# Binning: ranks summed on TensorE into one column per edge, copied out by ScalarE instead of reduced by VectorE

## The chip, the cores and the metric

The kernel runs on one core of a Trainium2 chip. The core has five engines that run their own instruction streams and meet at semaphores: TensorE (matrix products, written PE), VectorE (DVE), ScalarE (ACT), GpSimd (POOL) and SyncE (SP, which here issues the DMAs). The metric is the device time of one execution in microseconds.

## The reference

Two graph layers over 6250 nodes with 128 features and 200000 edges, sorted by destination. Cut to what matters:

```python
hij = concatenate([h[src], h[dst]]);  e = leaky_relu(hij @ w, 0.2) @ a
att = exp(e) / segment_sum(exp(e), src)[src]
x   = layernorm(x + segment_sum(h[src] * att, dst))          # layer 0
s   = exp(leaky(H_s[src] + H_t[dst]) - max)                  # layer 1, 4 heads
agg = segment_sum(s / (denom[src] + 1e-8) * H[dst], src) + x @ residual_projection
x   = layernorm(x + elu(agg))
```

Gathers and segment sums run over edges. The kernel first sorts the edges into bins, so that both become products with one-hot matrices.

## The kernel before, in words

The program runs through stages: constants, **binning** (`bin_windows`, line 109), edge scores, layer 0, norm and projection, layer 1, and the last norm. A stage ends with a barrier, so what it saves moves all that follows.

Binning goes over 49 windows of 4608 edges, 36 edges on each of 128 partitions. Nodes are in 49 blocks of 128. For each edge it needs the rank: the position of the edge among the edges of its window with the same source block. The rank of an edge is a sum of two parts: the count of edges in its block on the partitions above (*base*), and the count of equal keys among the edges before it on its own partition. One window n takes these steps:

- ScalarE `spread_key` (372, 376): copies the window's block numbers, each repeated 7 times, and its keys, each repeated 18 times, so that VectorE can compare runs.
- VectorE `find` (202, 210, 213): a one-hot of 49 blocks per edge (`bin_onehot`) and the equal-key table (`bin_same`).
- TensorE `base` (278): 36 matmuls add the one-hots of the partitions above; ScalarE `take_base` (382) copies the sum out.
- VectorE `pick` (223): one-hot times base, 36 x 49 numbers per partition (`bin_picked`), one of the 49 not zero.
- TensorE `rank` (288 to 306): with the identity as weights it adds the picked bases and the equal keys into PSUM. Seven columns per edge are kept: the 49 blocks are folded into 7 columns by seven matmuls of 252 columns, and the keys go into six or three of these columns, by ten matmuls.
- VectorE `sum_rank` (231): a reduction over the 7 columns, 252 numbers to 36 per partition, into `bin_rank_sum`.
- ScalarE `spread_rank` (402) repeats the ranks of 28 edges 8 times for VectorE `place` (238), which compares them with 128 lanes into `bin_lanes`. The ranks of the last 8 edges go through ScalarE itself, `measure_ranks` (388) and `place_late` (396).
- VectorE `fold` (245): one-hot times the two payloads (`bin_payload`). TensorE `fill` (317): 36 matmuls of lanes and payload put each edge into its slot. ScalarE `take_raw` (411, 412), TensorE `turn` (324), ScalarE `take_bytes` (418, 419), and SyncE stores the rows.
- Beside it, the projection of the node features runs block by block: `turn_x`, `project`, `take_off` on TensorE, `take_x`, `take_high`, `take_low` on ScalarE.

The windows are pipelined by an order that is written out by hand. In turn n VectorE does `find(n+2)`, `pick(n+1)`, `place(n)`, `fold(n)`, `sum_rank(n+1)`, and in every seventh turn `place_keys` for the seven windows to come. TensorE does `fill(n-1)`, `base(n+2)`, `turn_x(n+2)`, `take_off(n)`, `rank(n+1)`, `turn(n-1)`, `project(n+1)`. ScalarE does `measure_ranks(n)`, `take_raw(n-1)`, `place_late(n)`, `take_base(n+2)`, `spread_key(n+3)`, `take_x(n+2)`, `take_low(n)`, `spread_rank(n+1)`, `take_bytes(n-1)`, `take_high(n+1)`. `fill` waits for the payload and both parts of the lanes; `place` waits until `fill` of the window before has read the lanes; `pick` waits until `rank` of the window before has read what was picked; `rank` waits for `bin_same`, `bin_picked` and until the ranks before are out of PSUM. The base, rank and slots sums each have one PSUM bank.

Of the kernel before, what the change touches and what calls it, by code (L numbers as in the profile page):

```python
# [108 lines left out]
def bin_windows(nc, k, PQ, rows, wide_rows, src_rows, X, src, dst):  # L109
    NB, RING, E = NBK, 3, dst.shape[0]  # L110
    LANE_G, BLK_G, SUB_B, SUB_T, SPREADS = 8, 7, 7, 6, 4
# [4 lines left out]
    with Stage(nc) as ctx:  # L116
# [3 lines left out]
        def ps(name, shape, dt=F32):  # L120
            return ctx.enter_context(nc.psum_tensor(f"bin_{name}", shape, dt))
# [26 lines left out]
        rank_ps = ps("rank_ps", [P, 512])[:, 0:SUB_B * W_T].rearrange("p (t j) -> p t j", j=SUB_B)  # L148
# [9 lines left out]
        with nc.Block() as block:  # L158
# [21 lines left out]
            def _(dve):  # L180
# [45 lines left out]
                def sum_rank(n):  # L226
                    if n >= 2:
                        dve.wait_ge(s["rank_spread"], n - 1)
                        dve.wait_ge(s["away"], n - 1)
                    dve.wait_ge(s["ranked"], n + 1)  # L230
                    nc.vector.tensor_reduce(rank_sum[:, n % 2, :], rank_ps, AX.X, ALU.add).then_inc(s["rank_summed"], 1)

# [19 lines left out]
                for n in range(-2, NB + 1):  # L252
# [13 lines left out]
                    if 0 <= n + 1 < NB:  # L266
                        sum_rank(n + 1)
# [4 lines left out]
            def _(pe):  # L272
# [8 lines left out]
                def rank(n):  # L281
# [4 lines left out]
                    for b in range(0, NB, SUB_B):  # L286
                        w = min(SUB_B, NB - b)
                        nc.tensor.matmul(rank_ps[:, :, 0:w], k.ident_b[:], picked[:, :, b:b + w], start=(b == 0), stop=False)
                    eq, counts = same[:, n % 2, :], rank_ps.rearrange("p t j -> p j t")
                    for t in range(0, 18, SUB_T):  # L290
                        nc.tensor.matmul(counts[:, 0:SUB_T, 18:36], k.ident_b[:],
                                         eq[:, t * W_T:(t + SUB_T) * W_T].rearrange("p (i t) -> p i t", t=W_T)[:, :, 18:36],
                                         start=False, stop=False)
                    halves = eq.rearrange("p (h x) -> p h x", h=2)
                    for t in range(0, 9, 3):
                        nc.tensor.matmul(counts[:, 0:3, :].rearrange("p j (h c) -> p h j c", h=2)[:, :, :, 9:18], k.ident_b[:],
                                         halves[:, :, t * W_T:(t + 3) * W_T].rearrange("p h (i t) -> p h i t", t=W_T)[:, :, :, 9:18],
                                         start=False, stop=False)
# [64 lines left out]
            def _(act):  # L363
# [73 lines left out]
                for n in range(-2, NB + 1):  # L437
# [14 lines left out]
                    if 0 <= n + 1 < NB:  # L452
                        spread_rank(n + 1)
# [2035 lines left out]
```

## Time and profile before

| what | us |
|---|---|
| median of 3 runs | 3279.44 |
| the three | 3279.33, 3279.44, 3297.03 |
| profiled execution, its time | 3298.39 |
| its span | 3296.6 |
| TensorE busy in the span | 3064.1 (93%) |
| VectorE | 3045.2 (92%) |
| ScalarE | 2749.8 (83%) |
| mean granted TensorE clock | 0.965 |

The profile is one execution, and a slower one than the median. Busy shares of the whole span say little here, because the stages have different limits; the windows of the binning stage, 30.42 to 402.17 us, have to be read by themselves. A granted clock of 1.00 is 2.4 GHz and 0.50 is 1.2 GHz; values between are a mix of the two in time.

### The profile page before, as it was taken

The numbers are of one execution on the slowest core, as the hardware profiler recorded it, in microseconds if no ns is written. First come the engines' busy times: TensorE is split into PE (matmuls) and PEld (weight loads), VectorE is DVE, ScalarE is ACT, GpSimd is POOL, SyncE is SP. The second block draws the span as 40 slices with busy tenths as digits, with TensorE's granted clock in tenths as the row PEclk, the third lists the DMA queues.
The fourth block names the chain that finished last, engine by engine and source line by source line (L and its number), as shares of the span: only waits on it lengthen the run. The fifth ranks groups of instructions, "written<-read, shape, count | busy, mean of one in ns | idle before, by whom it ended". The sixth has DMA issues, their size and how long they took to land. (4 is left out here: it accounts for less than half of the span.)

```text
span 3296.6 us, 101505 instructions
## 1 busy us (share of the span) xinstructions
PE 3064.1 (93%) x40072; PEld 2795.8 (85%) x40072; DVE 3045.2 (92%) x4914; ACT 2749.8 (83%) x6951; POOL 155.1 (5%) x251
## 2 busy tenths in 40 slices
PE   5777699999999999699999999988999999999995
PEld 4666577777778777699999999988999999999993
DVE  8999889999999997799999999988999999999996
ACT  6988788888888885799999999976888888888886
POOL 0000000000000000000000000000111111111110
PEclk9988899999999997799999999998999999999998
DMA  2000022222222222233333333325554555555541
GB/s 66 13 13 12 10 103 93 92 86 92 93 91 93 92 87 47 65 97 97 97 97 97 96 97 96 97 58 162 161 163 160 163 163 161 162 164 163 160 141 41
DMA packets 173135, 333.06 MB, mean 101 GB/s; under 512 B 54860, under 2 KB 108704, under 8 KB 172576
## 3 DMA queue, kind: packets, MB, share of 16 engines
q1 hardware_dynamic: 170996, 323.30, 32.2%
q8 instruction: 322, 5.28, 0.6%
q10 hardware_dynamic: 1660, 3.20, 0.4%
q14 instruction: 157, 1.29, 0.1%
HBM read 320.77 MB, written 5.66 MB: 99 GB/s over the span
## 5 line engine op out<-in xcount | busy, mean ns | idle before, releaser
L987 PE MATMUL l_gathered<-xp,l_src_onehot 128*128 128x128 bf16 x7203 | 467.0, 221 | 11.2 <-DVE l_src_onehot L900 11.2
L1398 PE MATMUL l_gathered<-hp,l_onehot 128*128 128x128 bf16 x7203 | 458.9, 219 | 0.0
L682 PE MATMUL sc_z<-sc_onehot,pq 128*128 128x256 f32 (+1 forms) x2450 | 429.4, 298 | 27.6 <-DVE sc_leaky L595 18.3
L987 PEld LDWEIGHTS l_gathered<-xp,l_src_onehot 128*128 128x128 bf16 x7203 | 407.9, 99 | 26.4 <-DVE l_src_onehot L900 11.7
L766 ACT ACTIVATE sc_leaky<-sc_z 128x1024 f32<-128x1024 f32 (+3 forms) x325 | 309.4, 952 | 142.4 <-PE sc_z L686 139.5
L595 DVE SCALAR_TENSOR_TENSOR sc_leaky<-sc_z,sc_leaky 128x1024 f32<-128x1024 f32 (+3 forms) x325 | 370.1, 1139 | 59.9 <-ACT sc_leaky L766 52.3
L825 DVE TENSOR_TENSOR l_lane<-iota_b,l_lane_pairs 128x896 bf16<-128x896 bf16 x686 | 420.7, 613 | 0.0
L1398 PEld LDWEIGHTS l_gathered<-hp,l_onehot 128*128 128x128 bf16 x7203 | 406.6, 98 | 0.4
L686 PE MATMUL sc_z<-sc_onehot,pq 128*128 128x256 f32 (+1 forms) x2450 | 401.0, 286 | 0.0
L1412 PE MATMUL l_acc<-e,l_lane_wide 128*128 128x132 f32 x2744 | 385.3, 283 | 0.7 <-ACT e L1476 0.6
L682 PEld LDWEIGHTS sc_z<-sc_onehot,pq 128*128 128x128 f32 x2450 | 344.6, 196 | 40.2 <-issue 38.8
L686 PEld LDWEIGHTS sc_z<-sc_onehot,pq 128*128 128x128 f32 x2450 | 344.1, 195 | 0.0
L1307 DVE TENSOR_TENSOR e<-l_gathered,l_weight 128x768 f32<-128x768 f32 x343 | 325.5, 949 | 12.7 <-issue 9.0
L1412 PEld LDWEIGHTS l_acc<-e,l_lane_wide 128*128 128x128 f32 x2744 | 335.7, 190 | 1.6 <-ACT e L1476 1.0
L1465 ACT CAST l_lane_wide<-l_lane 128x896 fp32r<-128x896 bf16 x343 | 328.9, 959 | 0.0
L1033 ACT CAST l_lane_wide<-l_lane 128x896 fp32r<-128x896 bf16 x343 | 322.3, 940 | 4.0 <-DVE l_lane L825 4.0
L1470 ACT CAST l_message_halves<-e 128x396 fp32r<-128x396 f32 x343 | 179.1, 522 | 159.8 <-DVE e L1307 157.5
L998 PE MATMUL l_acc<-l_messages,l_lane_wide 128*128 128x128 f32 x2058 | 305.9, 285 | 5.7 <-ACT l_messages L1042 5.7
L587 DVE TENSOR_SCALAR sc_onehot<-placed,part 128x1536 fp32r<-128x1536 uint8 (+1 forms) x300 | 298.8, 997 | 3.4 <-DMA placed<-edge_rows 3.3
L1042 ACT ACTIVATE l_messages<-l_gathered,e 128x128 f32<-128x128 f32 x1029 | 300.5, 362 | 0.0
L914 DVE TENSOR_TENSOR l_message_halves<-l_messages,l_message_halves 128x512 fp32r<-128x512 f32 x343 | 237.3, 692 | 53.1 <-ACT l_message_halves L1048 48.0
L1476 ACT ACTIVATE e<-l_gathered,l_weight 128x32 f32<-128x32 f32 x1372 | 279.4, 285 | 0.0
(242 smaller groups left out, 6114.5 us busy)
## 6 DMA issues: line engine op xcount, KB each, us to landing
rows_got<-edge_rows_wide SPq DMA_DIRECT2D x343, 448.0 KB, 3.7
l_got<-edge_rows_src SPq DMA_DIRECT2D x343, 224.0 KB, 3.2
placed<-edge_rows SPq DMA_DIRECT2D x144, 512.0 KB, 3.7
out_dram<-X SPq DMA_DIRECT2D x12, 256.0 KB
edge_rows<-bin_bytes SPq DMA_DIRECT2D x98, 6.1 KB
edge_rows_wide<-bin_rows SPq DMA_DIRECT2D x98, 12.2 KB
sc_last_rows<-edge_rows SPq DMA_DIRECT2D x24, 64.0 KB, 3.5
placed<-edge_rows SPq DMA_DIRECT2D x6, 256.0 KB, 4.0
```

The lines of the kernel that those rows point to most:

```text
L595: nc.vector.scalar_tensor_tensor(out=y, in0=z, scalar=ALPHA, in1=y, op0=ALU.mult, op1=ALU.add).then_inc(s["leaky"], 1)
L682: nc.tensor.matmul(z[:, b, 0:nw, :], PQ[:, b0 + b, q, 0:C], hot[:, r % HOTS, b, 0, 0:nw, :], start=(b == u and q == 0), stop=False)
L686: ins = nc.tensor.matmul(z[:, u:u + v, n, :], PQ[:, 2 * pair + n, q, C:2 * C], hot[:, r % HOTS, u:u + v, 1, n, :], start=False, stop=(n == ...
L766: nc.scalar.activation(y, z, ACT.Relu, scale=1.0 - ALPHA).then_inc(s["positive"], 1)
L825: return nc.vector.tensor_tensor(out.rearrange("p i (u v) -> p i u v", v=2), k.iota_b[:].rearrange("p (u v) -> p u v", v=2).unsqueeze(1).t ...
L987: ins = nc.tensor.matmul(gps[:, t % 2, i * P:(i + 1) * P], hot[:, t % RING, i, :], parts[:, g * GX + i, q, :], start=(q == 0), stop=(q == 2))
L998: nc.tensor.matmul(acc[:, n % 2, 0:C], lane_wide[:, t % 2, i, :].bitcast(F32), msg[:, t % 2, i, :], start=(g == 0 and i == SPLIT), stop=Fa ...
L1033: nc.scalar.copy(lane_wide[:, t % 2], lane[:, t % 2]).then_inc(s["lane_wide"], 1)
L1307: nc.vector.tensor_tensor(msg[:, t % 2, 0:w, 0:C].rearrange("p i (e d) -> p i e d", e=HEADS), gps[:, t % 2, 0:w * P].rearrange("p (i e d) ...
L1398: ins = nc.tensor.matmul(gps[:, t % 2, i * P:(i + 1) * P], dst_hot[:, t % RING, i, :], hp[:, g * GX + i, q, 0:C], start=(q == 0), stop=(q ...
L1412: nc.tensor.matmul(acc[:, b % 2, 0:CW], lane_wide[:, t % 2, i, :].bitcast(F32), msg[:, t % 2, i, :], start=(g == 0 and i == SPLIT), stop=F ...
L1465: nc.scalar.copy(lane_wide[:, t % 2], lane[:, t % 2]).then_inc(s["lane_wide"], 1)
```

## The change

`rank` now sums into one column per edge. The 49 blocks are added by 49 matmuls of 36 columns, each of which reads one block's number for all 36 edges (every 49th element), and the keys by 35 matmuls of 18, 24, 12 or fewer columns. VectorE's `sum_rank` is gone. In its place ScalarE's `take_rank` copies the 36 sums out of PSUM, just ahead of `spread_rank` in ScalarE's order, behind the same waits.

```diff
--- before.py
+++ after.py
@@ -108,7 +108,7 @@
 
 def bin_windows(nc, k, PQ, rows, wide_rows, src_rows, X, src, dst):
     NB, RING, E = NBK, 3, dst.shape[0]
-    LANE_G, BLK_G, SUB_B, SUB_T, SPREADS = 8, 7, 7, 6, 4
+    LANE_G, BLK_G, SPREADS = 8, 7, 4
     HALF, LATE = W_T // 2, 8
     EARLY = W_T - LATE
     SAME, FIRST, SECOND = 37 * W_T, FIRST_WINDOWS, 4
@@ -145,7 +145,7 @@
         as_bytes, as_rows = sb("bytes", [P, 2, P], mybir.dt.uint8), sb("rows", [P, 2, P], BF16)
         xt = sb("x_turned", [P, 2, C])
         base_ps = ps("base", [P, 512])[:, 0:NB]
-        rank_ps = ps("rank_ps", [P, 512])[:, 0:SUB_B * W_T].rearrange("p (t j) -> p t j", j=SUB_B)
+        rank_ps = ps("rank_ps", [P, 512])[:, 0:W_T]
         slots_ps = ps("slots", [P, 512])[:, 0:2 * NB]
         turned = ps("turned", [P, 1024], BF16)[0:2 * NB, 0:P]
         xps = ps("x_turned_ps", [P, 512])[:, 0:C]
@@ -223,13 +223,6 @@
                     nc.vector.tensor_tensor(picked[:], oh[:, n % RING], base_sum[:].unsqueeze(1).to_broadcast([P, W_T, NB]),
                                             ALU.mult).then_inc(s["picked"], 1)
 
-                def sum_rank(n):
-                    if n >= 2:
-                        dve.wait_ge(s["rank_spread"], n - 1)
-                        dve.wait_ge(s["away"], n - 1)
-                    dve.wait_ge(s["ranked"], n + 1)
-                    nc.vector.tensor_reduce(rank_sum[:, n % 2, :], rank_ps, AX.X, ALU.add).then_inc(s["rank_summed"], 1)
-
                 def place(n):
                     if n >= 1:
                         dve.wait_ge(s["slots"], n)
@@ -263,8 +256,6 @@
                         place_keys(c, slice(0, CHUNK), read[c % 2], CHUNK * (c // 2 + 1) - (SECOND if c % 2 == 0 else 0), edges[:, c % 2])
                     if 0 <= n < NB:
                         fold(n)
-                    if 0 <= n + 1 < NB:
-                        sum_rank(n + 1)
                     if n == 0:
                         place_keys(0, slice(SECOND, CHUNK), read[0], CHUNK - SECOND, edges[:, 0])
 
@@ -283,27 +274,23 @@
                     pe.wait_ge(s["picked"], n + 1)
                     if n >= 1:
                         pe.wait_ge(s["rank_summed"], n)
-                    for b in range(0, NB, SUB_B):
-                        w = min(SUB_B, NB - b)
-                        nc.tensor.matmul(rank_ps[:, :, 0:w], k.ident_b[:], picked[:, :, b:b + w], start=(b == 0), stop=False)
-                    eq, counts = same[:, n % 2, :], rank_ps.rearrange("p t j -> p j t")
-                    for t in range(0, 18, SUB_T):
-                        nc.tensor.matmul(counts[:, 0:SUB_T, 18:36], k.ident_b[:],
-                                         eq[:, t * W_T:(t + SUB_T) * W_T].rearrange("p (i t) -> p i t", t=W_T)[:, :, 18:36],
-                                         start=False, stop=False)
+                    for b in range(NB):
+                        nc.tensor.matmul(rank_ps, k.ident_b[:], picked[:, :, b], start=(b == 0), stop=False)
+                    eq = same[:, n % 2, :]
+                    for t in range(18):
+                        nc.tensor.matmul(rank_ps[:, 18:36], k.ident_b[:], eq[:, t * W_T + 18:t * W_T + 36], start=False, stop=False)
                     halves = eq.rearrange("p (h x) -> p h x", h=2)
-                    for t in range(0, 9, 3):
-                        nc.tensor.matmul(counts[:, 0:3, :].rearrange("p j (h c) -> p h j c", h=2)[:, :, :, 9:18], k.ident_b[:],
-                                         halves[:, :, t * W_T:(t + 3) * W_T].rearrange("p h (i t) -> p h i t", t=W_T)[:, :, :, 9:18],
-                                         start=False, stop=False)
+                    for t in range(9):
+                        nc.tensor.matmul(rank_ps.rearrange("p (h c) -> p h c", h=2)[:, :, 9:18], k.ident_b[:],
+                                         halves[:, :, t * W_T + 9:t * W_T + 18], start=False, stop=False)
                     nines = eq.rearrange("p (h x) -> p h x", h=4)
-                    for t in range(0, 6, 3):
-                        nc.tensor.matmul(counts[:, 0:3, :].rearrange("p j (h c) -> p h j c", h=4)[:, :, :, t + 3:9], k.ident_b[:],
-                                         nines[:, :, t * W_T:(t + 3) * W_T].rearrange("p h (i t) -> p h i t", t=W_T)[:, :, :, t + 3:9],
-                                         start=False, stop=False)
+                    for t in range(6):
+                        c = t // 3 * 3 + 3
+                        nc.tensor.matmul(rank_ps.rearrange("p (h c) -> p h c", h=4)[:, :, c:9], k.ident_b[:],
+                                         nines[:, :, t * W_T + c:t * W_T + 9], start=False, stop=False)
                     threes = eq.rearrange("p (h x) -> p h x", h=12)
                     for t in range(2):
-                        ins = nc.tensor.matmul(counts[:, 0, :].rearrange("p (h c) -> p h c", h=12)[:, :, t + 1:3], k.ident_b[:],
+                        ins = nc.tensor.matmul(rank_ps.rearrange("p (h c) -> p h c", h=12)[:, :, t + 1:3], k.ident_b[:],
                                                threes[:, :, t * W_T + t + 1:t * W_T + 3], start=False, stop=(t == 1))
                     ins.then_inc(s["ranked"], 1)
 
@@ -394,6 +381,13 @@
                     if n >= 1:
                         act.wait_ge(s["slots"], n)
                     nc.scalar.activation(lanes[:, EARLY:W_T], far[:], ACT.Relu, scale=-1.0, bias=k.one_col[:]).then_inc(s["late_lanes"], 1)
+
+                def take_rank(n):
+                    if n >= 2:
+                        act.wait_ge(s["rank_spread"], n - 1)
+                        act.wait_ge(s["away"], n - 1)
+                    act.wait_ge(s["ranked"], n + 1)
+                    nc.scalar.copy(rank_sum[:, n % 2, :], rank_ps).then_inc(s["rank_summed"], 1)
 
                 def spread_rank(n):
                     if n >= 1:
@@ -450,6 +444,7 @@
                     if 0 <= n < NB:
                         take_low(n)
                     if 0 <= n + 1 < NB:
+                        take_rank(n + 1)
                         spread_rank(n + 1)
                     if n >= 1:
                         take_bytes(n - 1)
```

On VectorE, in the middle of the stage, a turn before (`bin_onehot`, `bin_same` are `find`, `bin_payload` is `fold`):

```order
L231 TENSOR_REDUCE bin_rank_sum<-bin_rank_ps 128x36
L202 TENSOR_TENSOR bin_onehot<-iota_b,e 128x1764
L210 TENSOR_TENSOR bin_same<-e,placed 128x18x18
L213 TENSOR_TENSOR bin_same<-e,placed 128x2x18x18
L223 TENSOR_TENSOR bin_picked<-bin_onehot,bin_base_sum 128x1764
L238 TENSOR_TENSOR bin_lanes<-iota_b,bin_rank 128x3584
L245 TENSOR_TENSOR bin_payload<-bin_onehot,e 128x36x49 x2
```

and now:

```order
L202 TENSOR_TENSOR bin_onehot<-iota_b,e 128x1764
L210 TENSOR_TENSOR bin_same<-e,placed 128x18x18
L213 TENSOR_TENSOR bin_same<-e,placed 128x2x18x18
L223 TENSOR_TENSOR bin_picked<-bin_onehot,bin_base_sum 128x1764
L231 TENSOR_TENSOR bin_lanes<-iota_b,bin_rank 128x3584
L238 TENSOR_TENSOR bin_payload<-bin_onehot,e 128x36x49 x2
```

The reduction is gone and nothing takes its place; the rest keeps its order.

On TensorE, from the base sums to the transpose of the slots, before:

```order
L278 MATMUL bin_base<-bin_onehot,above_b 128x49 x36
L331 MATMUL bin_x_turned_ps<-ident,X 128x128
L344 MATMUL bin_product<-pq,bin_negated 128x256
L288 MATMUL bin_rank_ps<-bin_picked,ident_b 128x252 x7
L291 MATMUL bin_rank_ps<-bin_same,ident_b 128x6x18 x3
L296 MATMUL bin_rank_ps<-bin_same,ident_b 128x2x3x9 x3
L301 MATMUL bin_rank_ps<-bin_same,ident_b 128x4x3x6
L301 MATMUL bin_rank_ps<-bin_same,ident_b 128x4x3x3
L306 MATMUL bin_rank_ps<-bin_same,ident_b 128x12x2
L306 MATMUL bin_rank_ps<-bin_same,ident_b 128x12
L324 MATMUL bin_turned<-ident_b,bin_raw 98x128
L337 MATMUL bin_product<-w_ext,bin_x_turned 128x256
```

and now:

```order
L269 MATMUL bin_base<-bin_onehot,above_b 128x49 x36
L318 MATMUL bin_x_turned_ps<-ident,X 128x128
L331 MATMUL bin_product<-pq,bin_negated 128x256
L278 MATMUL bin_rank_ps<-bin_picked,ident_b 128x36 x49
L281 MATMUL bin_rank_ps<-bin_same,ident_b 128x18 x18
L284 MATMUL bin_rank_ps<-bin_same,ident_b 128x2x9 x9
L289 MATMUL bin_rank_ps<-bin_same,ident_b 128x4x6 x3
L289 MATMUL bin_rank_ps<-bin_same,ident_b 128x4x3 x3
L293 MATMUL bin_rank_ps<-bin_same,ident_b 128x12x2
L293 MATMUL bin_rank_ps<-bin_same,ident_b 128x12
L311 MATMUL bin_turned<-ident_b,bin_raw 98x128
L324 MATMUL bin_product<-w_ext,bin_x_turned 128x256
```

Line 288 has become 278: 7 matmuls of 252 columns are 49 of 36, and the 10 of keys are 35.

On ScalarE, from the base copy to the next distances, now:

```order
L369 CAST bin_base_sum<-bin_base 128x49
L359 COPY e<-placed 128x252 x3
L363 COPY e<-placed 128x648
L419 COPY bin_x_turned<-bin_x_turned_ps 128x128
L427 CAST pq<-bin_product 128x256
L390 COPY bin_rank_sum<-bin_rank_ps 128x36
L396 CAST bin_rank<-bin_rank_sum 128x224
L412 COPY bin_rows<-bin_turned 98x128
L413 CAST bin_bytes<-bin_turned 98x128
L423 CAST pq<-bin_product 128x256
L375 ACTIVATE bin_away_from_rank<-iota_b,bin_rank_sum 128x128 x8
```

Line 390 is new. Before, line 402 (now 396) followed directly on the product copy (now 427).

## Rows read from the trace of the kernel before

**Rows 1.** Windows: busy us per engine (instructions), granted clock, DMA share, GB/s; binning stage

```profile
30.42:402.17 371.75, 275.11 (x4477) 237.10 (x4476) 365.24 (x434) 326.34 (x1058) 0.00 (x0) 0.91 0.07 12
```

**Rows 2.** VectorE in order of time (start, us, line, output<-inputs), one window of edges

```profile
199.10 1.19 DVE L202 TENSOR_TENSOR bin_onehot<-iota_b,e 128x1764 bf16<-128x1764 bf16 x1
...
201.86 2.01 DVE L238 TENSOR_TENSOR bin_lanes<-iota_b,bin_rank 128x3584 bf16<-128x3584 bf16 x1
203.80 2.31 DVE L245 TENSOR_TENSOR bin_payload<-bin_onehot,e 128x1764 bf16<-128x1764 bf16 x2
206.03 0.40 DVE L231 TENSOR_REDUCE bin_rank_sum<-bin_rank_ps 128x36 f32<-128x252 f32 x1
206.36 1.19 DVE L202 TENSOR_TENSOR bin_onehot<-iota_b,e 128x1764 bf16<-128x1764 bf16 x1
...
209.13 2.02 DVE L238 TENSOR_TENSOR bin_lanes<-iota_b,bin_rank 128x3584 bf16<-128x3584 bf16 x1
```

**Rows 3.** TensorE in order of time, the same window and the two behind it

```profile
202.04 1.13 PE L288 MATMUL bin_rank_ps<-bin_picked,ident_b 128*128 128x252 bf16 x7
203.00 0.44 PE L291 MATMUL bin_rank_ps<-bin_same,ident_b 128*128 128x108 bf16 x3
...
203.51 0.22 PE L306 MATMUL bin_rank_ps<-bin_same,ident_b 128*128 128x24 bf16 x2
203.57 0.24 PE L324 MATMUL bin_turned<-ident_b,bin_raw 128*98 128x128 bf16 x1
...
206.36 2.72 PE L317 MATMUL bin_slots<-bin_payload,bin_lanes 128*128 128x98 bf16 x36 [2.07 <-DVE bin_payload L245]
208.88 1.63 PE L278 MATMUL bin_base<-bin_onehot,above_b 128*128 128x49 bf16 x36
...
213.64 1.79 PE L317 MATMUL bin_slots<-bin_payload,bin_lanes 128*128 128x98 bf16 x36 [0.75 <-DVE bin_payload L245]
215.27 1.09 PE L278 MATMUL bin_base<-bin_onehot,above_b 128*128 128x49 bf16 x36
216.20 0.31 PE L331 MATMUL bin_x_turned_ps<-ident,X 128*128 128x128 f32 x1
```

**Rows 4.** Windows: two successive periods of the stage

```profile
199.10:206.36 7.26, 5.20 (x94) 4.41 (x95) 7.26 (x9) 6.78 (x22) 0.00 (x0) 1.00 0.04 9
206.36:213.63 7.27, 6.53 (x94) 5.83 (x95) 7.27 (x9) 6.78 (x22) 0.00 (x0) 0.77 0.10 15
```

**Rows 5.** ScalarE in order of time, the same window

```profile
203.86 0.20 ACT L382 CAST bin_base_sum<-bin_base 128x49 bf16<-128x49 f32 x1
203.94 1.02 ACT L372 COPY e<-placed 128x252 bf16<-128x252 bf16 x3
...
206.52 0.38 ACT L402 CAST bin_rank<-bin_rank_sum 128x224 bf16<-128x224 f32 x1 [0.49 <-DVE bin_rank_sum L231]
...
212.90 0.40 ACT L433 CAST pq<-bin_product 128x256 fp32r<-128x256 f32 x1
213.80 0.38 ACT L402 CAST bin_rank<-bin_rank_sum 128x224 bf16<-128x224 f32 x1 [0.50 <-DVE bin_rank_sum L231]
```

**Rows 6.** Groups by line, VectorE, whole stage: busy us, mean ns | idle before, releaser

```profile
L238 DVE TENSOR_TENSOR bin_lanes<-iota_b,bin_rank 128x3584 bf16<-128x3584 bf16 x49 | 98.8, 2017 | 5.8 <-PE bin_slots L317 5.7
...
L231 DVE TENSOR_REDUCE bin_rank_sum<-bin_rank_ps 128x36 f32<-128x252 f32 x49 | 20.1, 410 | 1.5 <-PE bin_rank_ps L306 1.5
```

**Rows 7.** TensorE in order of time, the first ranks, at the lower clock

```profile
27.78 1.68 PE L288 MATMUL bin_rank_ps<-bin_picked,ident_b 128*128 128x252 bf16 x7
29.27 0.49 PE L291 MATMUL bin_rank_ps<-bin_same,ident_b 128*128 128x108 bf16 x3
```

**Rows 8.** Windows: the stretch of the rows above, at its clock

```profile
27.78:29.55 1.77, 1.77 (x11) 1.25 (x10) 0.68 (x5) 1.19 (x5) 0.00 (x0) 1.00 0.22 30
```

**Rows 9.** Windows: where the scores end and the first layer begins

```profile
1274.00:1283.00 9.00, 9.00 (x77) 7.63 (x73) 5.57 (x10) 2.76 (x7) 0.00 (x0) 0.50 0.29 45
1283.00:1361.00 78.00, 56.40 (x488) 47.06 (x488) 49.74 (x82) 37.57 (x88) 0.00 (x0) 0.55 0.14 35
```

## The prediction

> **What bounds the kernel now.** I read first the windows of the whole span, to see which stage the diff touches. From 30.42 to 402.17 us, the binning stage, VectorE is busy 365.24 of 371.75 us, TensorE 275.11 and ScalarE 326.34, at a mean granted clock of 0.91 [rows 1]. Then VectorE's order of time inside one window of 4608 edges [rows 2]: `find`'s first comparison starts at 199.10 and that of the next window at 206.36, and nothing lies between its instructions. So VectorE's own work sets the period, 7.26 to 7.27 us. From the reduction's start at 206.03 to the next start at 206.36 is 0.33 us: that, not the 0.40 us that the row gives as its length, is what the reduction costs, because neighbours overlap by 0.07.
>
> TensorE comes next [rows 3]. It starts each window with `fill`, and stood idle before that for 2.07 us at 206.36 and 0.75 us at 213.64. The difference is the clock: 36 matmuls of 98 columns take 1.79 us at the high level (2.4 GHz, 213.64) and 2.72 us in a window in which part of it ran at 1.2 GHz (206.36). The windows by period show this as granted clock 1.00 with 5.20 us of TensorE work, and 0.77 with 6.53 [rows 4]. Last ScalarE [rows 5]: 6.78 of 7.27 us busy, and its one pause, 0.50 us, is before `spread_rank`, put down to the reduction. So the three engines would need, each alone, about 7.27 (VectorE), 6.7 (ScalarE, below) and 5.2 us (TensorE, high clock).
>
> **The change, part by part.**
>
> *VectorE loses the reduction.* 49 of them run [rows 6]. For 48 of them I take 0.33 us each off VectorE's period: 15.8 us. The first one waited 1.5 us for the first ranks [rows 6]; VectorE goes on to `find` of the third window during that time, and place of window 0 still needs the ranks, which come by then: 1.6 us. Together 17.4 us, and VectorE's period becomes 6.94.
>
> *TensorE: 84 matmuls of rank in place of 17.* The columns stay the same, 2394 per window (before 7x252 + 3x108 + 3x54 + 72 + 36 + 24 + 12; now 49x36 and the same rest). From the first at 202.04 to the transpose at 203.57 the old ones take 1.53 us [rows 3]. The new ones are short, and the nearest short ones are `base`: 36 of 49 columns take 0.93 us at the high clock, from 215.27 to 216.20, 26 ns each [rows 3]. For the 35 matmuls of keys 26 ns each: 0.9 us. The 49 of picked bases read one 2-byte element out of every 98 bytes, which no row shows. Bounds: 26 ns (as `base`), and 137 ns, what an old one takes for 36 runs of seven elements at the same 98-byte step (0.96 us for seven, 202.04 to 203.00). I take 31 ns. The reason is the first window, at 1.2 GHz: there seven of the 252-column matmuls take 1.49 us, 213 ns each, just 252 columns at 1.2 GHz (granted clock 0.50) [rows 7, 8], so the read with its jumps keeps up with one element per cycle of 1.2 GHz; 36 single elements at that pace are 30 ns. The last two old matmuls point the same way: 24 and 12 columns, in runs of two and of one element 216 bytes apart, start within 0.06 us [rows 3]. The new rank is then 49x31 + 0.9 = 2.4 us, 0.9 more than before. TensorE's work per window goes from 5.2 to 6.1 us, under 6.94, so it lies beside VectorE's. It is free as long as a picked matmul stays under (6.94 - 5.2 + 1.53 - 0.9) / 49 = 48 ns.
>
> The row and a rule stand against each other here. The Trainium skill (SBUF — State Buffer, section "Door 1: The DMA port swizzle (why `[64,N]` ≈ `[32,N]`)") says that SBUF is read in lines of 16 bytes, that full pace needs at least two hits in a line, and that each access which crosses to a new line pays. By it every one of the 36 elements pays, and the sum would stand or fall with the size of that payment, which the page doesn't give; this is the first rival below.
>
> *ScalarE gains one copy* of 128x36 from PSUM. Nearest: the 128x49 copy, 0.20 us long, whose follower starts 0.08 us after it [rows 5]. But `spread_rank` reads what the copy writes and waits for its end, so I count 0.20 plus some 0.05 for the signal. ScalarE's bare period before: `take_low` starts 212.90, lasts 0.40, and a follower may start 0.12 before the end, as at 203.94, so at 213.18; minus 206.52 is 6.66. Now 6.66 + 0.25 = 6.91, 0.03 under VectorE. This is tight. Bounds: 0.08 (as if nothing waited) and 0.45. Behind the copy in ScalarE's queue are `spread_rank`, two byte copies, `take_high` and the eight distances; VectorE's `place` waits for the first, and gets it over 2 us early. ScalarE no longer waits for VectorE there, but for TensorE, whose rank ends some 5.8 us after the payload, a microsecond before ScalarE comes to it.
>
> *What is late next.* `place` of a window needs the slots buffer that `fill` of the window before reads. At 206.36 `fill` started 0.25 us after the payload, took 2.72 and ended at 209.08; `place` started at 209.13 [rows 2, 3]: with a low clock there was already no slack. Now VectorE arrives 0.33 us earlier and gets nothing for it in such a window. About a fifth of the stage ran low (clock 0.91), some 9 of 48 windows: at most 3 us lost. But TensorE's pause at the high clock shrinks from 2.07 to about 0.8 us, and the clock fell after the long pauses, so I take half, 1.5 us.
>
> **Sum.** 17.4 - 1.5 = 16 us less. Against the profiled execution, 3298.39, that is 3282. The median of the times shown is 3279.44, 18.95 lower; the trace has TensorE at 1.2 GHz from 1274 to about 1361 us, where the later stages begin [rows 9], and one of the three times, 3297.03, stands where the profiled one does. The change doesn't touch that stretch. So I forecast 3279.4 - 16 = **3263**, and 3281 if the middle run is one like the profiled. What a measurement of this kernel can tell from no change is about 1%, 33 us.
>
> **Rivals.**
> - *The single-element read binds TensorE (slower).* Place: the 49 matmuls at line 288 of before. From 48 ns each TensorE's period passes VectorE's; at 55 ns nothing is gained; at 80 ns the period is 3.67 + 0.9 + 3.9 = 8.5 us, 1.2 over the old, and the kernel takes 3339; at 137 ns it would be 11.3, and 3476. For: 137 ns against 105 for 252 columns at 2.4 GHz. Against: the pace at 1.2 GHz. Chance 0.08, 0.05 of it over 1%. The Trainium skill's rule above would be this case.
> - *ScalarE becomes the bound.* With 0.45 us for the copy and its signal the period is 7.11: 0.16 a window, 7.5 us, 3272. For: its slack of 0.03. Against: ScalarE catches up 2 us in every seventh window, when VectorE prepares keys. Chance 0.14.
> - *The clock takes the gain.* If TensorE's low fifth stays or grows to a third, `place` waits in 16 windows: 5 us lost, 3267. Chance 0.08.
> - *More of the stage is freed*: with less idling TensorE stays high throughout and the waits of `place` before (5.7 us in all, 3 of them at the stage's end [rows 6]) go too: 3260. Chance 0.08.
> - My forecast, 3263 or its 3281: 0.62.
>
> The range, 3256 to 3285, holds all but the first rival. Faster by over 1% needs 33 us and has a chance only through which runs fall in the middle: 0.08. Slower by over 1% 0.06, within 1% 0.86.
>
> **What the profile after would show.** VectorE: no reduction, period near 6.94, no idle time before `find` or `pick`. TensorE: 49 matmuls in about 1.5 us, idle before `fill` near 0.8 us, granted clock over 0.91. ScalarE: a copy of 0.2 us, and little or no wait before it. I am wrong if VectorE waits for ranks or for slots in most windows, if the 49 take over 2.4 us, or if ScalarE shows no idle time and VectorE waits for spread keys.

## The result, and the profile after

The changed kernel takes **3405.13 us** (median of 6 runs, 3404.36 to 3406.05) against 3279.39 for the kernel before (6 runs, 3278.89 to 3297.03): ratio 1.0376, 95% interval 1.0356 to 1.0396. It is slower by 126 us, far above the range of 3256 to 3285. Runs of one kernel can fall in two groups some 19 us apart, and where they do below (e5, e7 and e8) both groups are given.

The windows of the changed kernel: per engine busy us (instructions), then granted clock, DMA share, GB/s. The first is the binning stage, the second one period inside it, the third all the rest.

```profile
30.00:527.23 497.23, 493.62 (x7752) 473.43 (x7750) 360.30 (x385) 346.60 (x1109) 0.00 (x0) 0.68 0.06 10
305.74:315.98 10.24, 10.24 (x162) 9.84 (x161) 7.21 (x8) 7.26 (x25) 0.00 (x0) 0.67 0.04 7
527.23:3402.70 2875.47, 2763.46 (x35496) 2538.50 (x35496) 2664.80 (x4424) 2418.36 (x5875) 153.88 (x245) 0.98 0.35 113
```

The stage ended at 402.17 before [rows 1] and ends at 527.23 now, 125.06 us later: the whole loss lies in it. In the place of a VectorE that is busy 365.24 of 371.75 us and a clock of 0.91 [rows 1] stands a TensorE that is busy 493.62 of 497.23 us at 0.68; VectorE has 137 us of idle time. A period is 10.24 us, against 7.26 and 7.27 [rows 4].

TensorE of the changed kernel in order of time (start us, us, engine, line, output<-inputs, count), one period:

```profile
305.74 3.15 PE L304 MATMUL bin_slots<-bin_payload,bin_lanes 128*128 128x98 bf16 x36
308.68 1.24 PE L269 MATMUL bin_base<-bin_onehot,above_b 128*128 128x49 bf16 x36
309.76 0.31 PE L318 MATMUL bin_x_turned_ps<-ident,X 128*128 128x128 f32 x1
309.82 0.36 PE L331 MATMUL bin_product<-pq,bin_negated 128*128 128x256 f32 x1
310.03 4.09 PE L278 MATMUL bin_rank_ps<-bin_picked,ident_b 128*128 128x36 bf16 x49
313.93 0.66 PE L281 MATMUL bin_rank_ps<-bin_same,ident_b 128*128 128x18 bf16 x18
314.44 0.39 PE L284 MATMUL bin_rank_ps<-bin_same,ident_b 128*128 128x18 bf16 x9
314.68 0.31 PE L289 MATMUL bin_rank_ps<-bin_same,ident_b 128*128 128x24 bf16 x6
314.84 0.21 PE L293 MATMUL bin_rank_ps<-bin_same,ident_b 128*128 128x24 bf16 x2
314.90 0.32 PE L311 MATMUL bin_turned<-ident_b,bin_raw 128*98 128x128 bf16 x1
315.02 1.17 PE L324 MATMUL bin_product<-w_ext,bin_x_turned 128*128 128x256 f32 x2
315.98 1.27 PE L304 MATMUL bin_slots<-bin_payload,bin_lanes 128*128 128x98 bf16 x13
```

No row has an idle time in brackets: TensorE goes from one step to the next. The 49 picked matmuls start at 310.03 and the keys at 313.93, so they take 3.90 us, **80 ns each** where seven old ones took 0.96 us together [rows 3]. The 35 matmuls of keys take 0.97 us. And `fill` takes 2.94 us from its start to the next (305.74 to 308.68), where at the high level it takes 1.63 (213.64 to 215.27 [rows 3]). The windows of `fill`, of about the first 12 of the 49 and of the last 12 show why:

```profile
305.74:308.68 2.94, 2.94 (x37) 2.94 (x36) 0.85 (x1) 2.94 (x11) 0.00 (x0) 0.50 0.10 20
310.03:311.00 0.97, 0.97 (x15) 0.97 (x14) 0.97 (x2) 0.97 (x4) 0.00 (x0) 1.00 0.00 0
313.00:313.93 0.93, 0.93 (x15) 0.93 (x13) 0.84 (x2) 0.00 (x0) 0.00 (x0) 0.50 0.00 0
```

The clock falls to 1.2 GHz during the scattered matmuls, stays there through the keys, the product of 315.02 and `fill`, and is back at 2.4 GHz when the next 49 begin. The scattered matmuls themselves take 80 ns at both levels.

VectorE of the changed kernel, the same period (in brackets the idle time before, and what ended it):

```profile
308.92 2.03 DVE L231 TENSOR_TENSOR bin_lanes<-iota_b,bin_rank 128x3584 bf16<-128x3584 bf16 x1 [2.33 <-PE bin_slots L304]
310.86 2.32 DVE L238 TENSOR_TENSOR bin_payload<-bin_onehot,e 128x1764 bf16<-128x1764 bf16 x2
313.27 1.21 DVE L202 TENSOR_TENSOR bin_onehot<-iota_b,e 128x1764 bf16<-128x1764 bf16 x1
315.09 0.33 DVE L210 TENSOR_TENSOR bin_same<-e,placed 128x324 bf16<-128x324 bf16 x1 [0.61 <-PE bin_rank_ps L293]
```

`place` (L231) waits 2.33 us for `fill` of the window before, and `find`'s second part (L210) 0.61 us for the ranks. Over the stage these waits are, by line, 104.5 us in the place of 5.8 [rows 6], and 25.8:

```profile
L231 DVE TENSOR_TENSOR bin_lanes<-iota_b,bin_rank 128x3584 bf16<-128x3584 bf16 x49 | 99.2, 2025 | 104.5 <-PE bin_slots L304 104.5
L210 DVE TENSOR_TENSOR bin_same<-e,placed 128x324 bf16<-128x324 bf16 x47 | 15.4, 327 | 25.8 <-PE bin_rank_ps L293 25.8
```

ScalarE of the changed kernel, the new copy and the instruction behind it:

```profile
315.17 0.19 ACT L390 COPY bin_rank_sum<-bin_rank_ps 128x36 f32<-128x36 f32 x1 [2.60 <-PE bin_rank_ps L293]
315.44 0.38 ACT L396 CAST bin_rank<-bin_rank_sum 128x224 bf16<-128x224 f32 x1
```

The copy takes 0.19 us, its reader starts 0.27 us after it started, and ScalarE idles 2.60 us before it.

### The profile page after: what moved, and what is told of

Same layout as the page of the kernel before. It is cut to its first block and busy times, and to the rows that moved or that the text cites. A ratio compares the mean times of both kernels' runs of the same rounds, so it can differ in the third digit from the quotient of the medians.

```text
span 3402.7 us, 108071 instructions
## 1 busy us (share of the span) xinstructions
PE 3265.2 (96%) x43355; PEld 3019.2 (89%) x43355; DVE 3041.1 (89%) x4865; ACT 2771.9 (81%) x7000; POOL 154.4 (5%) x251
## 5 line engine op out<-in xcount | busy, mean ns | idle before, releaser
L677 PE MATMUL sc_z<-sc_onehot,pq 128*128 128x256 f32 (+1 forms) x2450 | 419.4, 293 | 28.8 <-DVE sc_leaky L590 19.4
L681 PE MATMUL sc_z<-sc_onehot,pq 128*128 128x256 f32 (+1 forms) x2450 | 393.8, 282 | 0.0
L677 PEld LDWEIGHTS sc_z<-sc_onehot,pq 128*128 128x128 f32 x2450 | 334.3, 191 | 41.3 <-issue 39.9
L681 PEld LDWEIGHTS sc_z<-sc_onehot,pq 128*128 128x128 f32 x2450 | 337.9, 192 | 0.0
```

The lines of the kernel that those rows point to most:

```text
L677: nc.tensor.matmul(z[:, b, 0:nw, :], PQ[:, b0 + b, q, 0:C], hot[:, r % HOTS, b, 0, 0:nw, :], start=(b == u and q == 0), stop=False)
L681: ins = nc.tensor.matmul(z[:, u:u + v, n, :], PQ[:, 2 * pair + n, q, C:2 * C], hot[:, r % HOTS, u:u + v, 1, n, :], start=False, stop=(n == ...
```

## The experiments

The theory after this profile: one 2-byte element out of every 98 bytes costs 2.2 ns to read at either clock; that makes TensorE the bound, and the granted clock falls on top of it. Rivals: the count of short matmuls, or the new order of waits. The diffs are against the changed kernel, except e8's. In e1, e2, e3, e5, e6 and e11 the sums are not the ranks, so they have a further line that sets the flag of the count, and the program takes the same way whatever the ranks are. The other runs compute all that the reference asks.

**e1, the step of the read.** Seven windows each at steps of 2, 4, 8, 14, 16, 32 and 98 bytes.

```diff
-                    nc.tensor.matmul(rank_ps, k.ident_b[:], picked[:, :, b], start=(b == 0), stop=False)
+                    if n < 7:      # 2 bytes
+                        nc.tensor.matmul(rank_ps, k.ident_b[:], flat[:, b * 36:b * 36 + 36], start=(b == 0), stop=False)
...
+                    elif n < 21:   # 8 bytes
+                        nc.tensor.matmul(rank_ps, k.ident_b[:], flat[:, b * 32:b * 32 + 144:4], start=(b == 0), stop=False)
```

> The changed kernel, except that the 49 picked-base matmuls of 36 columns read the picked array at another step in every seven windows: 2, 4, 8, 14, 16, 32 and 98 bytes between elements. It leaves out that these sums are the ranks, and takes the binned path whatever the count says. Theory A (the read of one element per 16-byte line costs about 2.2 ns, whatever TensorE's clock): 26 to 31 ns a matmul at 2 and 4 bytes, under 45 at 8, near 80 at 14, 80 at 16, 32 and 98 bytes; the window's period is 6.94 us in the first 14 windows and about 10.2 us in the last 21. Theory B (any step other than one element costs the same): 80 ns already at 4 bytes. Theory C (the number of matmuls or their instructions is the cost): 80 ns at every step, 2 bytes too.

Measured: 3309.1 (one run). TensorE of e1 in order of time, at 2, 8, 14, 16 and 32 bytes; from the start of the 49 to the start of the keys (L295) is what they cost.

```profile
71.81 1.40 PE L280 MATMUL bin_rank_ps<-bin_picked,ident_b 128*128 128x36 bf16 x49
73.06 0.60 PE L295 MATMUL bin_rank_ps<-bin_same,ident_b 128*128 128x18 bf16 x18
...
153.06 1.95 PE L284 MATMUL bin_rank_ps<-bin_picked,ident_b 128*128 128x36 bf16 x49
154.84 0.61 PE L295 MATMUL bin_rank_ps<-bin_same,ident_b 128*128 128x18 bf16 x18
...
223.80 3.06 PE L286 MATMUL bin_rank_ps<-bin_picked,ident_b 128*128 128x36 bf16 x49
226.69 0.47 PE L295 MATMUL bin_rank_ps<-bin_same,ident_b 128*128 128x18 bf16 x12
...
272.89 3.46 PE L288 MATMUL bin_rank_ps<-bin_picked,ident_b 128*128 128x36 bf16 x49
276.16 0.62 PE L295 MATMUL bin_rank_ps<-bin_same,ident_b 128*128 128x18 bf16 x18
...
331.35 3.49 PE L290 MATMUL bin_rank_ps<-bin_picked,ident_b 128*128 128x36 bf16 x49
334.65 0.62 PE L295 MATMUL bin_rank_ps<-bin_same,ident_b 128*128 128x18 bf16 x18
```

Divided by 49: 26 ns at 2 bytes, 36 at 8, 59 at 14, 67 at 16 and at 32; 4 bytes gave 25.5 and 98 gave 79.6. So the count of matmuls is not the cost; the step is, at 36 columns each time. Theory A had the ends right, but forecast near 80 at 14, 16 and 32 bytes; why 98 bytes cost more than 16 or 32 no run shows. The Trainium skill (SBUF — State Buffer, section "Door 1: The DMA port swizzle (why `[64,N]` ≈ `[32,N]`)") says that reads want two hits in each line of 16 bytes, and that bf16 may be strided by up to 8 elements for free. The first half agrees with these rows in direction, the second doesn't: a step of 4 elements (8 bytes) already costs 36 ns for 26, and one of 8 elements (16 bytes) 67.

**e2, the same matmuls, contiguous.** All 49 read 36 contiguous columns, which are other numbers than the ranks need.

```diff
-                    nc.tensor.matmul(rank_ps, k.ident_b[:], picked[:, :, b], start=(b == 0), stop=False)
+                    nc.tensor.matmul(rank_ps, k.ident_b[:], flat[:, b * W_T:(b + 1) * W_T], start=(b == 0), stop=False)
```

> The changed kernel, except that each of the 49 matmuls reads 36 neighbouring elements of the picked array; it leaves out that the sums are the ranks, and takes the binned path whatever the count says. Theory A: the 49 take 49 x 26 to 31 ns = 1.3 to 1.5 us in place of 3.9, TensorE pauses again before fill, VectorE's period is 6.94 us and the kernel takes 3263 (3259 to 3268): all that the changed kernel lost and a gain of 16 over the kernel before. Theory C: the kernel stays near 3405. If ScalarE's chain becomes the bound: 3270 to 3275.

Measured: 3271.83 (3269.66 to 3276.80, 10 runs), ratio to before 0.9969 (0.9951 to 0.9987). One address pattern undone takes back all of the loss. But the gain over the 3279.39 of the kernel before is 7.6 us (7.1 over its 3278.93 in the runs beside e2), not 16. VectorE of e2 shows a period of 7.12 to 7.13 where 6.94 was forecast:

```profile
208.84 2.32 DVE L238 TENSOR_TENSOR bin_payload<-bin_onehot,e 128x1764 bf16<-128x1764 bf16 x2
211.25 1.21 DVE L202 TENSOR_TENSOR bin_onehot<-iota_b,e 128x1764 bf16<-128x1764 bf16 x1
```

From `fold` to `find` it is 2.41 us; before, from `fold` to the reduction, 2.23 [rows 2]. With three one-hot buffers, `find` writes the one that the `fold` just before it has read, so it waits for the end of the instruction directly ahead of it. The reduction had stood between them, and covered that.

**e5, e2 with a fourth one-hot buffer**, and **e8, the kernel before with one** (both: `RING` 3 to 4).

```diff
-    NB, RING, E = NBK, 3, dst.shape[0]
+    NB, RING, E = NBK, 4, dst.shape[0]
```

> e2_contiguous with four one-hot buffers in place of three; as there, the sums are not the ranks, and the binned path is taken whatever the count says. In e2_contiguous VectorE's period is 7.13 us and not 6.94: find starts 2.41 us after fold, where the reduction started 2.23 us after it. Theory D (find reuses the one-hot buffer that the fold just before it has read, and its wait for that fold costs 0.18 us, which the reduction used to cover): the period falls to 6.95, or to ScalarE's own chain of 6.97, and the kernel takes 3262 to 3265. Rival (ScalarE is the bound in e2_contiguous): period and time stay, 3270 to 3272.

> The kernel before with four one-hot buffers in place of three. Theory D: no difference (3279), since the reduction stands between fold and find and covers the wait. If the wait had cost something before too, up to 8 us less.

Measured: e5 3267.69 (10 runs, in two groups: 3262 to 3268 and 3281 to 3283), ratio 0.996 (0.9933 to 0.9988). e8 3279.94 (10 runs, in two groups: 3277 to 3280 and four of 3299), ratio 1.0003 (0.9972 to 1.0034). VectorE of e5:

```profile
198.81 1.20 DVE L202 TENSOR_TENSOR bin_onehot<-iota_b,e 128x1764 bf16<-128x1764 bf16 x1
...
203.51 2.32 DVE L238 TENSOR_TENSOR bin_payload<-bin_onehot,e 128x1764 bf16<-128x1764 bf16 x2
205.75 1.20 DVE L202 TENSOR_TENSOR bin_onehot<-iota_b,e 128x1764 bf16<-128x1764 bf16 x1
```

`find` now follows `fold` by 2.24 us and the period is 6.94, the forecast's number. The buffer is worth nothing to the kernel before, where the reduction stands in between. By medians e5 is 4.1 us faster than e2, less than the 9 that 0.18 us in 48 windows would be. The six lower runs of e5 have a median of 3264.1, 7.7 us under the ten of e2, which all lie between 3270 and 3277.

**e6, long but dense.** A first kernel for this question (e3) had 48 matmuls of 192 contiguous columns in place of the scattered ones, and gave no time. e6 is e2 and 34 matmuls of 192 contiguous columns more in each window, whose results nobody reads.

```diff
+                    for b in range(34):
+                        nc.tensor.matmul(rank_bank[:, 64:256], k.ident_b[:], flat[:, b * 32:b * 32 + 192], start=False, stop=False)
```

> e2_contiguous with 34 more matmuls of 192 neighbouring columns per window, each 80 ns at 2.4 GHz, whose sums nobody reads; the sums are not the ranks, and the binned path is taken whatever the count says. TensorE has 8.5 us of work per window at the high clock, as much as the changed kernel has by its 80 ns matmuls, but dense. Theory A1 (the changed kernel lost 60 us by the 80 ns and the other 66 us by a clock that falls although TensorE never stands idle, because the scattered matmuls use the array little): the clock stays at 0.95 or over, the period is 8.5 us, the kernel takes about 3339. Theory A2 (the clock falls for any TensorE stream of this length): clock near 0.67, over 3400.

Measured: 3314.01 (3312.79 to 3319.01, 9 runs), ratio 1.0077 (1.0052 to 1.0102). Windows of e6, and one of the changed kernel and of e2 beside it:

```profile
200.00:300.00 100.00, 100.00 (x2344) 97.55 (x2342) 88.76 (x97) 83.65 (x278) 0.00 (x0) 1.00 0.08 14
```

```profile
200.00:300.00 100.00, 100.00 (x1583) 95.98 (x1581) 73.44 (x83) 69.73 (x223) 0.00 (x0) 0.66 0.07 12
```

```profile
200.00:300.00 100.00, 79.25 (x2149) 73.92 (x2148) 98.24 (x107) 92.21 (x305) 0.00 (x0) 0.95 0.08 15
```

e6 and the changed kernel have a TensorE that never pauses, and the first keeps its clock at 1.00, with a period of 8.32 us, while the second has 0.66 and 10.24. The clock stayed, as theory A1 has it; its time of 3339 was 25 us too long. So TensorE as the bound costs 42 us (e6 less e2), and the lower clock the other 91 (changed kernel less e6).

**e9 and e10, dense work added to the scattered.** The changed kernel with a matmul of 192 contiguous columns after every seventh (e9) or every fourth (e10) of the 49.

```diff
+                        if b % 7 == 6:   # e10: b % 4 == 3
+                            nc.tensor.matmul(rank_bank[:, 64:256], k.ident_b[:], flat[:, b * 32:b * 32 + 192], start=False, stop=False)
```

> The changed kernel with work added: behind every seventh of the 49 scattered matmuls one more of 192 neighbouring columns (80 ns at 2.4 GHz), seven per window, whose sums nobody reads. It computes all that the reference asks. Theory A1 (the clock falls because the array is used little during the 3.9 us of scattered matmuls): if seven dense ones are enough, the clock stays near 1.00, the period is 8.3 + 0.6 = 8.9 us in place of 10.24, and the kernel gets faster by adding work, about 3340; if they are not enough, the clock stays at 0.67 and each costs its time, about 3430. Theory A2 (what the array is given makes no difference): about 3430 or more.

> As e9_extra7, with the dense matmul behind every fourth scattered one, twelve per window. Theory A1: clock near 1.00, period 8.3 + 1.0 = 9.3 us, about 3360; where seven weren't enough and twelve are, this one is the faster of the two. Theory A2: over 3440.

Measured: e9 3402.74 (3399.68 to 3404.73), ratio 1.0357 (1.0312 to 1.0402); e10 3406.31 (3405.62 to 3407.22), ratio 1.0371 (1.0327 to 1.0416), 4 runs each. Windows of e9, then of e10:

```profile
200.00:300.00 100.00, 100.00 (x1659) 96.26 (x1657) 74.55 (x83) 68.36 (x223) 0.00 (x0) 0.84 0.08 13
```

```profile
200.00:300.00 100.00, 100.00 (x1702) 96.24 (x1700) 74.37 (x83) 68.37 (x222) 0.00 (x0) 0.84 0.07 13
```

Seven or twelve extra matmuls cost nothing: the clock rises from 0.66 to 0.84 and gives back what they take. The period of both is still 10.24 us. No theory had this time: A1 said 3340 and 3360 with a clock near 1.00, A2 3430 and more. In these runs the clock goes with what TensorE streams and not with how busy the profile shows it; why the period keeps its value stays open.

**e12 and e13, the same work in another order of TensorE's.** e12 splits the 49 into 17, 16 and 16, with `base` and the keys between them; e13 sends 36 of them one by one between the matmuls of `base`.

```diff
+                    if 0 <= n + 1 < NB:
+                        add_picked(n + 1, slice(0, 17))
...
+                    if 0 <= n + 1 < NB:
+                        add_picked(n + 1, slice(17, 33))
```

> The changed kernel with nothing but TensorE's order changed: the 49 scattered matmuls of a window stand in three lots of 17, 16 and 16, with the 36 base matmuls of the window after next between the first two and x's turn, the product and 18 key matmuls before the third. Same instructions, same sums. Theory A1 (the clock falls behind an unbroken stretch of 3.9 us in which the array is used little): broken into lots of 1.3 us the clock rises, the period falls from 10.24 towards 8.3, the kernel takes 3320 to 3360. Theory A3 (the period is held at 10.24 as in the two kernels with more work, where the clock rose to 0.83 and the time stayed): clock above 0.67, time 3400 to 3406. Theory A2 (the order makes no difference): clock 0.67, 3405.

> The changed kernel with TensorE's order changed alone: 36 of the 49 scattered matmuls stand one by one between the 36 base matmuls of the window after next. Same instructions, same sums. Theory A1: one stretch again, 4.9 us long and a little denser (26 ns of base behind each 80 ns), so the clock is between those of the changed kernel and of e12_split: 3340 to 3400. If the scattered read is hidden behind the base matmul, whose own read comes from elsewhere: 80 ns for the pair in place of 106, and up to 45 us less than that. Theory A2: clock 0.67, 3405.

Measured: e12 3377.62 (3372.11 to 3377.84, 4 runs), ratio 1.0293 (1.0276 to 1.031). e13 3407.69 (3405.82 to 3408.64, 4 runs), ratio 1.0389 (1.0372 to 1.0407). The windows of e12:

```profile
100.00:200.00 100.00, 98.99 (x1739) 95.23 (x1736) 79.45 (x89) 77.74 (x251) 0.00 (x0) 0.88 0.07 12
200.00:300.00 100.00, 100.00 (x1710) 96.27 (x1710) 79.75 (x85) 75.12 (x243) 0.00 (x0) 0.81 0.06 11
300.00:400.00 100.00, 100.00 (x1594) 95.67 (x1592) 73.54 (x77) 72.81 (x232) 0.00 (x0) 0.70 0.05 10
```

The order alone takes back 27.5 us. It is less than A1 said (3320 to 3360), and the clock sinks from 0.88 to 0.70 over these windows. VectorE of e12 shows a period in which TensorE kept 2.4 GHz (granted clock 1.00 from 227.02 to 235.20): `place` at 227.02 and at 235.20, 8.18 us.

```profile
227.02 2.03 DVE L231 TENSOR_TENSOR bin_lanes<-iota_b,bin_rank 128x3584 bf16<-128x3584 bf16 x1 [2.25 <-PE bin_slots L308]
...
235.20 2.02 DVE L231 TENSOR_TENSOR bin_lanes<-iota_b,bin_rank 128x3584 bf16<-128x3584 bf16 x1 [0.45 <-PE bin_slots L308]
```

e13 has the clock (0.66) and the time that A2 gives, by which the order makes no difference: spread one by one among the `base` matmuls the scattered ones lose as much as in one stretch, so what in e12's order helps is not shown. In e13 a scattered matmul and one of `base` together take 106 ns (80 + 26): nothing of the jumps hides behind another matmul.

**e4 and e7, layouts that compute the whole.** VectorE writes the picked bases in groups of seven blocks (e4, TensorE reads at a step of 14 bytes) or in pairs (e7, 4 bytes).

```diff
-        picked = sb("picked", [P, W_T, NB], BF16)
+        picked = sb("picked", [P, NB // BLK_G, W_T, BLK_G], BF16)
...
-                        nc.tensor.matmul(rank_ps, k.ident_b[:], picked[:, :, b], start=(b == 0), stop=False)
+                        nc.tensor.matmul(rank_ps, k.ident_b[:], picked[:, b // BLK_G, :, b % BLK_G], start=(b == 0), stop=False)
```

> The changed kernel with the picked array laid out as seven groups of blocks, in each of which the 36 edges lie 14 bytes apart; VectorE writes it in runs of seven, TensorE reads one element out of 14 bytes. It computes all that the reference asks. Theory A (cost per 16-byte line): most elements still lie on a line of their own, so 70 to 80 ns a matmul and 3385 to 3405. If the price goes by the distance jumped and 14 bytes are cheap: about 3263 plus what VectorE's scattered write costs (pick 1.09 us before; every 0.1 us more is 5 us).

> The changed kernel with the picked array laid out in pairs of blocks: in each pair the 36 edges lie 4 bytes apart. TensorE reads at 4 bytes, 25 ns a matmul as in the ladder; VectorE writes pairs 144 bytes apart and needs one more small instruction for the 49th block. It computes all that the reference asks. If pairs keep VectorE's pace (1.09 us for pick, some 0.1 for the extra one): period 7.2, 3276. If VectorE falls to the pace of e4_groups (1.72 us): period 7.9, 3308.

Measured: e4 3306.15 (3305.86 to 3311.48, 4 runs), ratio 1.0087 (1.007 to 1.0103). e7 3311.82 (6 runs in two groups, about 3302 and 3321), ratio 1.0076 (1.0035 to 1.0116). The matmuls take 59 and 26 ns, but VectorE pays for writing in short runs: `pick` takes 1.72 us in e4 (1.09 before), and in e7 1.71 and 0.21.

```profile
203.06 1.71 DVE L223 TENSOR_TENSOR bin_picked<-bin_onehot,bin_base_sum 128x1728 bf16<-128x1728 bf16 x1
204.60 0.21 DVE L227 TENSOR_TENSOR bin_picked<-bin_onehot,bin_base_sum 128x36 bf16<-128x36 bf16 x1
```

On the engine that bounds, that is more than the reduction had cost (0.33). e4 is far from the 3385 to 3405 of its theory A, since 14 bytes cost 59 ns and not 70 to 80; e7's second alternative, 3308, came. No version of the change that computes the ranks beats the kernel before.

**e11, runs.** 36 columns out of the same 98-byte rows, as 36 single elements, 18 runs of two, 12 of three, 9 of four, twelve windows each (thirteen of the last).

```diff
+                        elif n < 24:
+                            nc.tensor.matmul(rank_ps.rearrange("p (t v) -> p t v", v=2), k.ident_b[:], picked[:, 0:18, c:c + 2], start=(b == 0), stop=False)
```

> The changed kernel, except that from window 12 on the 36 columns of a picked-base matmul are read as 18 runs of two, from window 24 on as 12 runs of three, from window 36 on as nine runs of four neighbouring elements, the runs always 98 bytes apart; there it leaves out that the sums are the ranks, and it takes the binned path whatever the count says. Theory E (the price is one of 2.2 ns per jump, behind which the other elements of a run are hidden; a run of seven hides it all but for 1 ns, which is why the old matmuls looked cheap): 80, 40, 27 and 25 ns, the last two at the floor of short matmuls. Rival (price per element read in a scattered pattern): 80 ns for all.

Measured: 3299.36 (one run). TensorE of e11 with runs of two and of three, in order of time:

```profile
175.05 2.45 PE L282 MATMUL bin_rank_ps<-bin_picked,ident_b 128*128 128x36 bf16 x49
177.32 0.62 PE L289 MATMUL bin_rank_ps<-bin_same,ident_b 128*128 128x18 bf16 x18
...
273.43 1.68 PE L284 MATMUL bin_rank_ps<-bin_picked,ident_b 128*128 128x36 bf16 x49
274.94 0.61 PE L289 MATMUL bin_rank_ps<-bin_same,ident_b 128*128 128x18 bf16 x18
```

That is 46 and 31 ns; single elements take 80, runs of four 26, the floor of short matmuls. Per run it is 2.2, 2.6, 2.6 and 2.9 ns, the last at the floor, where 80, 40, 27 and 25 ns were forecast: what is paid is in the main the jump, and most of a run passes during it. A run of seven takes 3.8 ns (137 / 36 [rows 3]), more than either a jump or seven elements at 2.4 GHz (2.9), so not all of it.

## Why the prediction was wrong, step by step

- **The step that failed: "the read with its jumps keeps up with one element per cycle of 1.2 GHz", 31 ns a picked matmul.** It is 80 ns, 2.2 ns an element. The 213 ns on which I built came from runs of seven: seven elements take 5.8 ns at 1.2 GHz, which is longer than a jump of 2.2 ns, so the pace would look the same with the jump or without it. A run that hides a cost can't bound it. The other witness, old matmuls of 24 and 12 columns that start within 0.06 us, was too short to tell: 12 jumps at 2.2 ns are 26 ns, what the shortest matmuls take anyway. The number that spoke against it, 137 ns for 252 columns that are 105 at 2.4 GHz, was the sign that the jumps cost something once the elements pass faster. I also put that stretch at a granted clock of 0.50; [rows 8] says 1.00, so the row does not carry the sentence. The `base` matmuls ahead of it take 42 ns each (23.99 to 25.50 for 36) for 26 at the high level, which fits 1.2 GHz; which it was stays open.
- **The first rival's mechanism was right**, which had the chance 0.08. Its 3.9 us for the 49 and 0.9 for the keys (0.97, and 0.88 at the high clock in e1) came. The rest of TensorE's work, from start to start, is 3.4 us and not 3.67 (5.2 of busy time less 1.53); so its period at 2.4 GHz is 8.18 us (e12) for 8.5, and the free limit some 54 ns for 48. e1 agrees: a period of 7.12 us at 36 ns, as in e2, and 7.6 at 67 where the clock holds. Its time, 3339, is 66 us short, the balance of two errors. It took TensorE at the high clock, which leaves out 98 us (below). And it counted 1.2 us in every window, where the turns with VectorE's keys, 9.68 us for 7.27 in the kernel before, cost next to nothing once TensorE bounds (9.16 and 7.54 in e6 for two of 8.32), six times 2.4 us.
- **The clock.** I reasoned that shorter pauses keep TensorE at the high level. The pauses are gone and the granted clock fell from 0.91 to 0.68. The Trainium skill (TensorE: Matmul & The Clock Gate, section "What's actually happening") says that the clock follows how busy TensorE has been. By the profile's busy share the rows contradict it (100% at 0.66, e6 100% at 1.00). Whether TensorE counts as busy while it waits for a scattered read no run shows: e6 and e9 would fit that it doesn't, and e12 and e13, the same matmuls at 0.81 and 0.66, show that it is not all. So what the lower clock costs is shown, and why it fell is open.
- **The reduction, 0.33 us a window and 17.4 in all**: mis-sized. With a fast read the period fell by 0.14 (e2, 7.6 us in all), since `find` had to wait for `fold` directly ahead of it; I had moved `find` up to `fold` without asking who frees its buffer. With a fourth buffer the 6.94 comes (e5).
- **ScalarE**: 0.19 us and a signal of 0.08 were forecast as 0.20 and 0.05. In e5 its turn takes 6.96 to 6.97 us without a pause, not 6.91, so it stands 0.02 to 0.03 over VectorE's 6.94 and not under it; still VectorE does not wait for it there. That rival did not come, but by less than was forecast.
- **`place` waits for slots** was named as what is late next, for 9 windows and 3 us. It came in all windows, 104.5 us. That, and over 2.4 us for the 49, are two of the signs of being wrong that the prediction named.

So the sum of the loss: -7.6 (reduction, e2), +42 (TensorE the bound at full clock; e6 had some 0.15 us a window more work than the changed kernel, so some 35 of it are the change's), +91 (clock; 98 then). It gives 126. The changed kernel's own rows agree on the clock: against e6 its period has 1.31 us more in `fill`, 0.47 in the product, 0.15 in `base` and 0.14 in the keys and `turn`, 2.07 in 48 windows, or 99 us.

## What to carry to other kernels

A matmul's moving operand that takes single elements out of rows costs the jump, not the column: bound it from a row that reads single elements, since a run of several hides most of it. Before an instruction is taken from between two others on the bounding engine, ask what it covered: here a buffer wait of 0.18 us, half the gain. When TensorE comes to be the bound, price it at the clock that its stream will be granted, and not at the clock it had.

## What the runs showed that was not expected

- TensorE shown busy 100 of 100 us at a granted clock of 0.66 (changed kernel), 0.84 with dense matmuls added at no cost (e9, e10), 1.00 with a dense stream (e6).
- The scattered read takes the same 80 ns per 36 elements at either level, as the changed kernel (49 in 3.90 us, the clock falling on the way) and e9 (49 and seven dense ones in 4.50 us, at a granted clock of 1.00 throughout) show.
- A little more on each read can cost the clock: in e1 the windows at 32 bytes (67 ns) have a granted clock of 0.88 and periods of 7.6 to 9.7 us, those at 98 bytes (80 ns) 0.66 and about 10.3.
- VectorE writes 1764 bf16 elements in 1.09 us when contiguous and in 1.72 us in runs of seven (e4); 1728 in runs of two take 1.71 (e7).
- The order of TensorE's instructions alone moved the kernel by 27.5 us (e12), and another order by 2.6 (e13).
